# Two mixture-of-experts stages around linear attention: edges of the expert stages rearranged, slots computed inside the steps, the first gathers moved forward

## The reference, cut to what matters

```python
x = x + 0.5 * ffn(layernorm(x)); x = x + attn(layernorm(x)); x = x + 0.5 * ffn(layernorm(x))

def ffn(x, wg, w1, b1, w2, b2):              # N = 4096 tokens, M = 128, E = 8 experts, K = 2, H = 512
    capacity = K * N // E                    # 1024 rows for each expert
    topv, topi = top_k(softmax(x @ wg), K);  topv /= sum(topv)
    pos = running count of each expert's tokens, all first choices before all second choices
    valid = pos < capacity;  gate = topv * valid
    disp[topi, pos] += x * valid             # E x capacity rows
    y = relu(disp @ w1 + b1) @ w2 + b2
    return sum over k of gate * y[topi, pos]

def attn(x):                                 # 16 heads of 8, linear attention, 8 sequences of 512
    q, k = elu(x@Wq.T + bq) + 1, elu(x@Wk.T + bk) + 1;  v = x@Wv.T + bv
    return ((q @ (k^T v)) / clip(q . sum(k), 1e-6)) @ Wo.T + bo
```

## Time and profile before

| | us |
|---|---|
| three runs | 512.05, 512.68, 510.95 (median 512.05) |
| profiled execution, its own time | 511.76 |
| its span, first to last instruction | 509.9 |
| TensorE busy | 331.7 (65%) |
| VectorE busy | 339.5 (67%) |
| ScalarE busy | 236.2 (46%) |
| GpSimd busy | 270.9 (53%) |

### The profile page before, as it was taken

One profiled execution on the slowest core, in us unless ns is written; L12 is line 12 of the kernel. 1 busy time (PEld: TensorE's weight loads), 2 busy tenths in 40 slices (PEclk: granted clock), 3 DMA queues, 4 the chain that ended last, 5 costly groups with the idle time before them and its releaser, 6 DMA issues. The chain is left out here.

```text
span 509.9 us, 5878 instructions
## 1 busy us (share of the span) xinstructions
PE 331.7 (65%) x1679; PEld 266.7 (52%) x1679; DVE 339.5 (67%) x1035; ACT 236.2 (46%) x430; POOL 270.9 (53%) x302
## 2 busy tenths in 40 slices
PE   7913489999999205678779830000479999999600
PEld 6902178888888103556657710000458888888400
DVE  6788579888787325689989782000057888888673
ACT  3687056666666103456548451000046666666200
POOL 9000777655630077667650737777603666666730
PEclk9999999999999755799988955555589999999955
DMA  8920114665554412112110101111131222221399
GB/s 238 356 90 0 37 50 145 194 187 183 188 189 158 163 51 53 47 46 53 42 42 1 54 22 52 52 54 52 51 127 36 84 81 82 84 63 41 117 335 282
DMA packets 43632, 53.32 MB, mean 105 GB/s; under 512 B 6646, under 2 KB 27152, under 8 KB 43600
## 3 DMA queue, kind: packets, MB, share of 16 engines
q1 hardware_dynamic: 30720, 33.69, 20.2%
q0 software_dynamic: 8512, 17.15, 11.6%
q10 hardware_dynamic: 4368, 2.10, 1.4%
HBM read 25.52 MB, written 27.39 MB: 104 GB/s over the span
## 5 line engine op out<-in xcount | busy, mean ns | idle before, releaser
L981 ACT ACTIVATE hf<-psum,bcol 128x512 f32<-128x512 f32 x128 | 88.5, 692 | 65.5 <-PE psum L918 62.4
L890 POOL DMA_INDIRECT xg<-xn_dram,gidx x64 | 65.1, 1017 | 68.1 <-POOLq L1541 38.0
L880 POOL DMA_INDIRECT yt_dram<-y_sb,target x64 | 70.3, 1099 | 51.8 <-DVE y_sb L1031 36.5
L1018 DVE TENSOR_TENSOR hl<-hf,hh 128x512 fp32r<-128x512 f32 x128 | 87.0, 692 | 4.5 <-ACT hh L983 2.0
L1118 POOL DMA_INDIRECT yg<-y_dram,slot x64 | 60.7, 949 | 25.1 <-issue 18.7
L916 PE MATMUL psum<-xh,wres 128*128 128x512 f32 x128 | 54.9, 429 | 2.8 <-DVE xl L1007 2.8
L1007 DVE TENSOR_TENSOR xl<-psum,xh 128x512 fp32r<-128x512 f32 x32 | 21.9, 684 | 51.9 <-ACT xh L966 51.9
L966 ACT CAST xh<-psum 128x512 fp32r<-128x512 f32 x32 | 18.8, 588 | 75.9 <-PE psum L904 73.7
L929 PE MATMUL psum<-hh,wres 128*128 128x512 f32 x128 | 52.8, 413 | 0.0
L918 PE MATMUL psum<-xh,wres 128*128 128x512 f32 x128 | 51.6, 403 | 0.0
L917 PE MATMUL psum<-xl,wres 128*128 128x512 f32 x128 | 51.6, 403 | 0.0
(11 more groups left out here) (221 smaller groups left out, 734.6 us busy)
## 6 DMA issues: line engine op xcount, KB each, us to landing
yt_dram<-zeros SPq DMA_DIRECT2D x24, 256.0 KB, 3.4
ring<-yt_dram SPq DMA_DIRECT2D x24, 256.0 KB, 5.0
xs_dram<-blank SPq DMA_DIRECT2D x16, 260.0 KB, 3.1
xg<-xs_dram SPq DMA_DIRECT2D x16, 260.0 KB, 2.7
wexp_raw<-in_L_ffn_w SPq DMA_DIRECT2D x16, 256.0 KB, 6.0
y_dram<-y_sb SPq DMA_DIRECT2D x16, 256.0 KB, 2.4
x_sb<-in_L_attn_x SPq DMA_DIRECT2D x8, 256.0 KB, 4.0
xn_dram<-xns SPq DMA_DIRECT2D x8, 256.0 KB, 6.2
```

The costliest lines, as they stand in the source:

```text
L880: gp.indirect_dma_start(out=yt_dram, out_offset=bass.IndirectOffsetOnAxis(ap=target[:, j:j + 1], axis=0), in_=self.y_sb[:, s % YG, t], in_ ...
L890: gp.indirect_dma_start(out=self.xg[:, s % 4, t], out_offset=None, in_=xn_dram, in_offset=bass.IndirectOffsetOnAxis(ap=gidx[:, j:j + 1], a ...
L981: one = nc.scalar.activation(self.hf[:, c], bank[1 + c][:], ACT.Relu, bias=bcol[:, at:at + 1])
L1018: dve.tensor_tensor(self.hl[:, s % 2, c], self.hf[:, c], self.hh[:, s % 2, c].bitcast(F32), ALU.subtract).then_inc(hl_ready[c], 1)
```

## The change

- *Order of superblocks.* turn(1), high(1) and low(1) move behind all four chunks of superblock 0 (chunk HC-1 instead of chunk 0), in both expert stages. In up, the matmul that reads xl goes from second to third place, and the wait for it stands before that one.
- *Weight rests.* weights_low(0) alone stands before superblock 0; step s < 7 makes weights_low(s+1).
- *Slots and gates* become a generator that is advanced by two yields in each step from 8 on; the slots raise slots_in_y.
- *First gathers.* Gather's batch 0 is issued by GpSimd at the end of block 2, once the slots are known and y is stored; its tile yg is allocated outside the block and has two buffers (YB) instead of four.
- *Clears.* xs_dram is cleared with zeros (blank is gone); yt_dram is cleared at two parts a step. yt_dram has one spare row for each slot ahead of its three parts; targets_of turns a target of zero into the slot's own spare row with two VectorE instructions instead of one.
- *WARM* is 50 instead of 36.

```diff
@@ -44,7 +44,7 @@
 RING = 8
-WARM = 36
+WARM = 50
 YG = 4
@@ -109,7 +109,7 @@
         xs_dram = nc.dram_tensor("xs_dram", (2 * E * CAP + N, XW), F32, kind="Internal").ap()
-        yt_dram = nc.dram_tensor("yt_dram", (3 * N + YG * SEQ, C), F32, kind="Internal").ap()
+        yt_dram = nc.dram_tensor("yt_dram", (E * CAP + 3 * N, C), F32, kind="Internal").ap()
 
@@ -134,8 +134,9 @@
         block_mask = sb("block_mask", [P, P])
-        zeros = sb("zeros", [P, GT, C])
-        blank = sb("blank", [P, YG, GT, XW])
+        zeros = sb("zeros", [P, GT, XW])
+        spare_row = sb("spare_row", [P, E * NCH])
+        aimed = sb("aimed", [P, E * NCH])
         ones_row = sb("ones_row", [2, P])
@@ -778,18 +771,44 @@
 
-                bias_pairs(dve, ch)
-                ch.then(dve.tensor_scalar(valid[:], at[:], float(CAP), None, ALU.is_lt))
-                ch.then(dve.tensor_tensor(slotf[:], at[:], valid[:], ALU.mult))
-                ch.then(dve.tensor_tensor(slot[:].rearrange("p k t -> p (k t)"), slotf[:], base[:], ALU.add))
+                def then(ins):
+                    ch.add(ins)
+                    return ch.n
+
+                dve.wait_ge(small_in[1], 16 * 6)
+                done = then(dve.tensor_copy(bhi[:], brow[:]))
+                yield
+                ch.wait(done)
+                done = then(dve.tensor_tensor(blo[:], brow[:], bhi[:].bitcast(F32), ALU.subtract))
+                yield
+                ch.wait(done)
...
+                done = then(dve.tensor_scalar(valid[:], at[:], float(CAP), None, ALU.is_lt))
+                yield
+                ch.wait(done)
+                done = then(dve.tensor_tensor(slotf[:], at[:], valid[:], ALU.mult))
+                yield
+                ch.wait(done)
+                dve.tensor_tensor(slot[:].rearrange("p k t -> p (k t)"), slotf[:], base[:], ALU.add).then_inc(slots_in_y, 1)
+                yield
 
                 dve.wait_ge(exp_gap, f + 1)
                 vk = lambda k: valid[:, k * NT:(k + 1) * NT]
-                ch.then(dve.tensor_scalar(total[:], e2[:], 1.0, None, ALU.add))
-                ch.then(dve.reciprocal(gap[:], total[:]))
+                done = then(dve.tensor_scalar(total[:], e2[:], 1.0, None, ALU.add))
+                yield
+                ch.wait(done)
+                done = then(dve.reciprocal(gap[:], total[:]))
+                yield
+                ch.wait(done)
                 ch.add(dve.scalar_tensor_tensor(gate[:, 0], gap[:], 0.5, vk(0), ALU.mult, ALU.mult))
-                ch.then(dve.tensor_tensor(e2[:], e2[:], gap[:], ALU.mult))
-                ch.then(dve.scalar_tensor_tensor(gate[:, 1], e2[:], 0.5, vk(1), ALU.mult, ALU.mult))
+                done = then(dve.tensor_tensor(e2[:], e2[:], gap[:], ALU.mult))
+                yield
+                ch.wait(done)
+                ch.add(dve.scalar_tensor_tensor(gate[:, 1], e2[:], 0.5, vk(1), ALU.mult, ALU.mult))
 
@@ -812,14 +831,13 @@
             def sync(self, sp):
-                sp.wait_ge(blank_ready, 1)
                 for s in range(2, self.STEPS):
 
                     sp.wait_ge(y_ready, self.b + s - 1)
                     sp.dma_start(rows(y_dram, (s - 2) * 512), self.y_sb[:, s % 2]).then_inc(y_stored[s % 2], 16)
-                    sp.dma_start(token_rows(xs_dram, (s - 2) * SEQ), blank[:, s % YG]).then_inc(xs_cleared, 16)
-                    for part in range(3 * (s - 2) // 2, 3 * (s - 1) // 2):
-                        sp.dma_start(token_rows(yt_dram, part * SEQ), zeros[:]).then_inc(yt_cleared, 16)
+                    sp.dma_start(token_rows(xs_dram, (s - 2) * SEQ), zeros[:]).then_inc(xs_cleared, 16)
+                    for part in range(2 * (s - 2), min(2 * (s - 1), 3 * NG)):
+                        sp.dma_start(token_rows(yt_dram, E * CAP + part * SEQ), zeros[:].rearrange("p t c -> p (t c)")[:, 0:GT * C].rearrange("p (t c) -> p t c", c=C)).then_inc(yt_cleared, 16)
                 for u in range(2):
@@ -849,7 +867,7 @@
                         sp.wait_ge(yt_added, i - RING + 1)
-                    sp.dma_start(self.ring[:, i % RING], token_rows(yt_dram, part * N + g * SEQ)).then_inc(yt_in[i % RING], 16)
+                    sp.dma_start(self.ring[:, i % RING], token_rows(yt_dram, E * CAP + part * N + g * SEQ)).then_inc(yt_in[i % RING], 16)
 
@@ -907,15 +925,17 @@
                     if c == 0:
-                        pe.wait_ge(xl_ready, b + s + 1)
+                        pe.wait_ge(xh_ready, b + s + 1)
                         if b == 0 and s % 2 == 0:
                             pe.wait_ge(exp_lo, s // 2 + 1)
                     if b + s > 0:
                         pe.wait_ge(hf_ready[c], b + s)
                     at = slice(c * P, (c + 1) * P)
                     nc.tensor.matmul(bank[1 + c][:], w[:, 0, at], self.xh[:, s % 2], start=True, stop=False)
-                    nc.tensor.matmul(bank[1 + c][:], w[:, 0, at], self.xl[:, s % 2], start=False, stop=False)
-                    nc.tensor.matmul(bank[1 + c][:], w[:, 2, at], self.xh[:, s % 2], start=False, stop=True).then_inc(h_ready[c], 1)
+                    nc.tensor.matmul(bank[1 + c][:], w[:, 2, at], self.xh[:, s % 2], start=False, stop=False)
+                    if c == 0:
+                        pe.wait_ge(xl_ready, b + s + 1)
+                    nc.tensor.matmul(bank[1 + c][:], w[:, 0, at], self.xl[:, s % 2], start=False, stop=True).then_inc(h_ready[c], 1)
 
@@ -955,7 +975,7 @@
                             down(s - 1, c)
-                        if c == 0 and s + 1 < NSB:
+                        if c == (HC - 1 if s == 0 else 0) and s + 1 < NSB:
                             turn(s + 1)
@@ -1019,8 +1039,10 @@
 
+                    js = slice(GT * s, GT * s + GT)
                     dve.wait_ge(slot_rows_in[s % XG], 16 * (s // XG + 1))
-                    dve.tensor_copy(target[:, GT * s:GT * s + GT], self.xg[:, s % XG, :, C + 1]).then_inc(targets_known, 1)
+                    ch.then(dve.scalar_tensor_tensor(aimed[:, js], self.xg[:, s % XG, :, C + 1], 0.0, spare_row[:, js], ALU.is_equal, ALU.mult))
+                    dve.tensor_tensor(target[:, js], aimed[:, js], self.xg[:, s % XG, :, C + 1], ALU.add).then_inc(targets_known, 1)
 
@@ -1039,17 +1061,17 @@
                 if b == 0:
-                    for e in range(E // 2):
-                        weights_low(e)
+                    weights_low(0)
                 low(0)
+                slots_and_gates = Route.slots_and_gates(dve, ch, self.f)
                 if b > 0:
                     targets_of(0)
                 for s in range(self.STEPS):
                     here = s < NSB
-                    if b == 0 and s < E // 2:
-                        weights_low(E // 2 + s)
-                    if b == 0 and s == NSB:
-                        Route.slots_and_gates(dve, ch, self.f)
+                    if b == 0 and s < E - 1:
+                        weights_low(s + 1)
+                    if b == 0 and s >= E:
+                        advance(slots_and_gates, 2)
                     if here:
@@ -1059,7 +1081,7 @@
                         h_low(s, 0)
-                    if s + 1 < NSB:
+                    if 1 <= s < NSB - 1:
                         low(s + 1)
@@ -1069,6 +1091,10 @@
                         h_low(s, 3)
+                    if s == 0:
+                        low(1)
+                        if b > 0:
+                            targets_of(1)
 
@@ -1098,7 +1124,7 @@
 
-        YB = 4
+        YB = 2
 
@@ -1107,16 +1133,25 @@
 
+            def batch(self, gp, n):
+
+                for k in range(K):
+                    if n >= 1:
+                        gp.wait_ge(yg_used[k], n)
+                    for t in range(GT):
+                        gp.indirect_dma_start(out=self.yg[:, n % YB, k, t], out_offset=None, in_=y_dram,
+                                              in_offset=bass.IndirectOffsetOnAxis(ap=slot[:, k, GT * n + t:GT * n + t + 1], axis=0)).then_inc(yg_in[k][n % YB], 16)
+
+            def first(self, gp):
+
+                gp.wait_ge(slots_in_y, 1)
+                for u in range(2):
+                    gp.wait_ge(y_stored[u], 16 * NSB // 2)
+                self.batch(gp, 0)
+
             def gpsimd(self, gp):
-                f = self.f
-                for n in range(NG):
-                    G = NG * f + n
-                    for k in range(K):
-                        if f == 0 and n >= 1:
-                            gp.wait_ge(yg_used[k], G)
-                        for t in range(GT):
-                            gp.indirect_dma_start(out=self.yg[:, n % YB, k, t], out_offset=None, in_=y_dram,
-                                                  in_offset=bass.IndirectOffsetOnAxis(ap=slot[:, k, GT * n + t:GT * n + t + 1], axis=0)).then_inc(yg_in[k][n % YB], 16)
+                for n in range(1, NG):
+                    self.batch(gp, n)
 
@@ -1536,6 +1571,8 @@
 
+        yg_stage = ExitStack()
+        gather = Gather(yg_stage, 0)
         raw_stage = ExitStack()
```

(8 more changed lines are left out.)

13 lines of the change are left out of this document (6 added, 7 removed).

## The result

| | median us | runs, lowest to highest |
|---|---|---|
| before, on the same chip | 512.12 | 10, 510.93 to 513.90 |
| changed | 507.33 | 10, 506.11 to 509.92 |

The ratio is 0.9916 with a 95% interval from 0.9894 to 0.9938: 4.8 us less, where 4.9 was forecast. The profiled execution took 507.46 us (span 505.7; before 511.76 and 509.9).

The account below looks back on a forecast made before the run. It took TensorE to bound the expert stages and GpSimd's gathers and scatters to pace attention's start and the dispatch. Terms: -5.2 by the dispatch, +0.3 at the second stage, -4.9 from 512.05: 507.1 us, range 504.6 to 510.8.

Parts of the forecast that it names:

- First stage's start: First expert stage: fewer early splits, waiting for xh only and the new superblock order gain 2.4 us, bounds 1.0 to 3.2.
- Splits: First stage's start: with only one weight split ahead, GpSimd's first gathers run freer, 1.2 us less.
- The xh-only wait: First matmul of superblock 0 waits for xh only, with xl's subtraction beside two matmuls: 0.75 us less.
- pause of 1 to 2 us: Expected sign in the first stage: TensorE pauses between superblock 0's twelve matmuls and superblock 1's first, near 67.3.
- b1's rival: For b1: gathers pace the first stage's start in either order, so the old order costs 0 to 0.5 us more.
- First stage's end: Last transposes no longer wait for y's copy behind slot and gate instructions: 0.3 us gained, bounds 0 and 1.17.
- First gathers: Edge to attention: first gather 6.2 us earlier; all wait for GpSimd at the block's end, batch 1's gathers 4.4 earlier.
- Attention: From batch 1's gathers to the dispatch's second part: VectorE can catch up, keeping between 4.4 and 5.9 us.
- attention stays at the low clock: Slower rival: TensorE's clock rises later in attention, each slow batch costs 2.9 us; 515.9 with three; chance 7%.
- -5.2 at the dispatch: Total gain expected at the dispatch's second part (301.88), 2.7 of it the first stage's own.
- Second stage's start: Fifty transposes keep the clock full, but the new order exposes a chain: first down matmul at 380.0, 0.3 us lost.
- The rule on transposes: Second stage: by it the 50 transposes run at low clock, ending at 375.1; rival total 511.1, chance 3%.

Follow-up runs that it names:

- b2: The changed kernel with four weight splits ahead of superblock 0 and one in each of steps 0 to 3, as before; 508.88 us, ratio 0.995.
- f1: The changed kernel with superblock 1's old order in the second expert stage alone; 505.35 us, ratio 0.9885 to the kernel before.
- b1: The changed kernel with superblock 1 behind chunk 0 again in the first expert stage alone; 509.4 us, ratio 0.9953 to the kernel before.
- b3: The changed kernel with all slot and gate instructions at the start of step 16 again; 509.84 us, ratio 0.9938 to the kernel before.
- a2: The changed kernel with GpSimd waiting at the first expert block's end until batch 0's gathers have landed; 511.41 us, ratio 0.9982.
- a1: The changed kernel with batch 0's gathers issued in the attention block again; 509.56 us, ratio 0.9924 to the kernel before.
- c2: The changed kernel with batch 0's gathers in the attention block and yt_dram cleared three parts in two steps again; 511.43 us, ratio 0.9985.
- d1: The changed kernel with superblock 1's old order in the second stage and weight split s made in step s (1 to 7); 505.73 us, ratio 0.9854.
- e1: The kernel before with 50 instead of 36 transposes ahead of the second stage, nothing else; 512.24 us, ratio 1.0005.
- a4: The changed kernel with 36 instead of 50 transposes ahead of the second stage; 509.85 us, ratio 0.9947 to the kernel before.

## Why the prediction was right, and where its terms were not

*First stage's start.* Forecast 2.4 (1.0 to 3.2); by superblock 3's transposes it is 2.04 (25.84 to 23.80). Splits: 1.2 forecast, 1.01 measured at the first row transposes (7.76 to 6.75 behind the first gather), and b2 agrees. The xh-only wait: 0.75 forecast, 0.72 measured (1.40 to 0.68). Both together: the first matmul 1.73 earlier, forecast 1.97.

In the order of superblock 1, the "pause of 1 to 2 us" came (1.33), and the first matmul of superblock 1, forecast near 67.3, came at 65.41. Of that block 1 has 1.09; the rest is that the matmuls are 0.43 apart only until 61.88 and 0.23 at 62.95 to 63.18. These are the distances that go with a granted clock of 0.50 (before, 374.71 to 375.14) and 1.00 (before, 379.68 to 379.91); the clock column itself can't be used here, for it shows 1.00 from the start of every profile until its first recorded fall. The earlier full speed bought nothing: in f1 all twelve are 0.43 apart (the last at 65.30), and superblock 2's transposes come 17.84 behind the first gather, as in the changed kernel (17.82), which waits there for gathers. One of those was held up by a moved split (1.89 at 59.88), for which the prediction had no term. So b1's rival fits better than the forecast: the order's own part of the 2.4 is not shown to be more than 0.

*First stage's end.* 0.3 forecast; 0.36 between the kernels (1.80 to 1.44 from yT to the copy). With the slots back at the end (b3) 0.08 of it is lost, so its cause is only partly these instructions, and that the size holds is luck.

*First gathers: the step that failed.* "GpSimd then issues all eight gathers inside the block ... and everyone waits for it at the block's end", and so "batch 1's gathers wait until the first rows are used". Neither happens. In the changed kernel the ninth gather is 6.7 earlier, not 4.4, 1.1 of it block 1's; counted from y's last copy it is 3.3 instead of 1.7. a2 makes GpSimd hold the block's end, and that costs 3.2 us at the ninth gather and 4.1 in the median, about 2.0 of it for the landing, which the prediction did not assume. The first gather itself was right: 3.5 earlier forecast behind y's last copy (6.2 less the stage's 2.7), 3.3 measured. Its parts, taken off one after the other: 1.1 the early issue (a1), 1.4 the clears (c2), 0.8 open. The prediction had the three clears in view and gave them no term of their own.

*Attention.* Forecast: all of 4.4 to 5.9 kept, the lead growing. The lead is 6.85 at the dispatch's first scatter (279.31 to 272.46) and 5.33 at its second part:

```profile
296.55 1.03 POOL L763 DMA_INDIRECT xs_dram<-xns,place  x1 [9.04 <-DVE xns L743]
```

(301.88 in the earlier trace rows). The 1.5 between was lost in one place. VectorE's kk of the seventh batch is 6.86 ahead (267.90, before 274.76), that of the eighth 5.20 (277.98, before 283.18). Between the two the granted clock of the changed kernel fell (0.57 from 270 to 274), where before had 1.00, and the eight matmuls at 270.17 took 1.89 instead of 1.16. TensorE's last pause ahead of the fall was 0.50 us, at 268.65; before it was 0.56, and the clock stayed. It is near the rival "attention stays at the low clock", but here it fell again. From the dispatch's first scatter to its second part eleven of the twelve profiles of changed kernels take 24.02 to 24.24 us; d1, e1 and before take 22.57 to 22.59. Over the whole stretch its size can't be told from chance: from the ninth gather to the second part it took 116.38 in e1, whose attention is that of before (113.73), and 114.20 to 116.50 in kernels with the changed one.

So -5.2 at the dispatch was hit (5.33) by luck. Of it 1.09 is block 1's, which isn't the change's (the stage's first gather scatters from 50.55 to 51.85 over all profiles); the change's own part in these two profiles is 4.24, below the 4.4 that was its lower bound. The gathers brought 1.6 more than forecast, the first stage 0.4 less and attention 2.2 less.

*Second stage's start.* 7.9 forecast, 8.20 measured, 7.62 before. The chain named (last activations, cast, VectorE, xl(1)) is the one that delays. Two things stood wrong inside it: as far as e1 and a4 show, the clock is kept by the shorter wait and not by the 50 transposes, and "only exposes a chain" hid a price. With the full clock the old order takes 5.64, so the new one costs 2.6 us; the net 0.6 is that less the 2.0 that the clock and the shorter wait give. I compared with a trace in which the clock was low, and never worked out what the old order would do with it full. No run tells of the two gather buffers, the spare rows or the second instruction for the targets, which were forecast at nothing.

*The rule on transposes.* The Trainium skill (TensorE: Matmul & The Clock Gate, PE-mode transpose) says that transposes don't count as busy for the clock the same way. In all profiles here, as in the earlier trace rows, the clock rises with nothing but transposes on TensorE: in a4 it is at full from 363, 4 us after the first. The trace decides.

## What to carry to other kernels

Ask of every reordering at a stage's edge what the old order would do once the other edits of the change are in: two edits can hide each other's price, as here 2.0 gained and 2.6 lost at one place. (f1 takes only the second one back: 5.64 us instead of 8.20.) What a block's end waits for is worth reading in the trace before it is priced: two clears fewer behind the last store brought 1.4 us, and taking the gathers out from behind the block's end 1.1 more. And a difference under 0.5% between variants of this kernel does not show in medians of six runs; it shows in marks inside the profile, where several profiles of the same code agree on them.

## What the runs showed of the hardware

- Engines left the block while GpSimd's queue held gathers that it had yet to issue (VectorE's add at 177.72, GpSimd's entry at 181.11); a wait on their landing in GpSimd's own stream (a2) put the first add at 15.6 us behind y's last copy instead of 10.15.
- No one length of a pause on TensorE decided whether the granted clock fell. Behind four row transposes at the second stage's start 1.40 us brought it from 1.00 to 0.50 (before, e1), and 0.68 did not in any of the twelve profiles that have it. Behind twelve matmuls and four transposes it fell in d1 (1.40 us, to 0.53) and a1 (1.39), and did not in c2 (1.39) and in the changed kernel (1.33 and 1.40); what separates these cases is open.
- One stretch of unchanged code in attention varied by 2.7 us between executions (113.73 and 116.38), with the clock at 1.00 or 0.87 between 220 and 240.
- The first stage's eighth indirect gather took 1.87 to 1.98 us in the ten profiles in which a weight split (128x1024) on VectorE began 0.04 to 0.16 us ahead of it, and 0.94 in the three in which the two began within 0.02 us (a1, b1, c2); there the split took 1.27 or 1.28 instead of 1.21 or 1.22.
